# Reordering the prologue of an fp32 transformer block: DMA queue order, and which engine makes which small split

## The reference

```python
mod = silu(c) @ wmod                      # six rows of 128 per batch: sa, ca, ga, sb, cb, gb
h = layernorm(x) * (1 + ca) + sa
q, k, v = h @ (w * scale)                 # 16 heads of 64
a = (q + q_bias) @ k.T / 8 + relative_causal(q @ emb.T / 8)
a = softmax(where(causal, a, -1e9))
x = x + ga * ((a @ v) @ out_kernel + out_bias)
h = layernorm(x) * (1 + cb) + sb
x = x + gb * top1_moe(h)                  # 16 experts, capacity 256, 128 -> 512 -> 128
```

## Time and profile before

| what | value |
|---|---|
| time of the launch, median of 3 runs | 904.1 us (903.34 to 904.54) |
| time of the profiled execution | 906.07 us |
| its span | 904.0 us |
| mean TensorE clock granted | 0.991 |
| PE busy | 875.8 us, 97% |
| ACT busy | 710.3 us, 79% |
| DVE busy | 665.9 us, 74% |
| POOL busy | 518.7 us, 57% |

### The profile page before, as it was taken

One profiled execution on the slowest core, in us unless ns is written; L12 is line 12 of the kernel. 1 busy time (PEld: TensorE's weight loads), 2 busy tenths in 40 slices (PEclk: granted clock), 3 DMA queues, 4 the chain that ended last, 5 costly groups with the idle time before them and its releaser, 6 DMA issues.

```text
span 904.0 us, 17653 instructions
## 1 busy us (share of the span) xinstructions
PE 875.8 (97%) x5632; PEld 702.2 (78%) x5632; DVE 665.9 (74%) x2053; ACT 710.3 (79%) x1970; POOL 518.7 (57%) x786
## 2 busy tenths in 40 slices
PE   6999999999999999999999999999999999997994
PEld 5777777887777778777777877777887777766994
DVE  4778778787878687777878787868777677753884
ACT  4788888888888888888888888888888888841551
POOL 2455555565565755675557556675566556633354
PEclk9899999999999999999999999999999999999998
DMA  7000790000000000000000000000000000006671
GB/s 271 2 1 1 190 243 24 1 19 18 13 1 2 36 1 13 1 28 10 13 1 15 12 13 1 2 21 8 5 1 22 2 13 1 9 22 218 215 213 39
DMA packets 23068, 38.92 MB, mean 43 GB/s; under 512 B 3094, under 2 KB 16135, under 8 KB 22592
## 3 DMA queue, kind: packets, MB, share of 16 engines
q1 hardware_dynamic: 19184, 29.11, 11.1%
q0 software_dynamic: 3072, 5.94, 1.8%
q10 hardware_dynamic: 720, 2.75, 0.9%
HBM read 23.44 MB, written 16.82 MB: 45 GB/s over the span
## 4 chain that ended last, share of the span: by engine, by line
PE 86%; DVE 1%; POOL 1%; DMA 1%; issue 1%; ACT 1%; POOLq 0%; DVEq 0%
PE bank L773 21%; PE bank L803 16%; PE bank L738 15%; PE bank L783 14%; PE bank L810 5%; PE bank L759 4%; PE bank L770 3%; PE bank L981 2%; PE bank L970 2%; DMA x<-xbuf 1%; PE bank L831 1%; POOL out L443 1%; PE bank L961 0%; PE bank L818 0%; PE bank L825 0%
## 5 line engine op out<-in xcount | busy, mean ns | idle before, releaser
L395 POOL TENSOR_SCALAR prob<-prob,rsum 128x128 f32<-128x128 f32 (+3 forms) x512 | 263.1, 532 | 238.4 <-DVE rsum L1101 232.4
L553 ACT ACTIVATE prob<-srow,nmax 128x512 f32<-128x512 f32 (+3 forms) x512 | 286.3, 560 | 66.5 <-DVE nmax L1089 63.7
L1089 DVE CUSTOM_DVE_ANT_0 srow<-bank,consts 128x512 f32<-128x512 f32 (+3 forms) x512 | 247.0, 488 | 98.0 <-issue 76.4
L783 PE MATMUL bank<-consts,prob 128*128 128x128 f32 x1280 | 201.7, 272 | 0.2 <-POOL prob L395 0.2
L783 PEld LDWEIGHTS bank<-consts,prob 128*128 128x128 f32 x1280 | 158.4, 140 | 22.9 <-POOL prob L395 0.5
L388 POOL TENSOR_TENSOR qlo<-qx,qhi 128x384 fp32r<-128x384 f32 x128 | 129.5, 1012 | 54.5 <-ACT qhi L518 53.2
L562 ACT ACTIVATE pt<-bank 128x384 f32<-128x384 f32 x318 | 153.3, 495 | 5.4 <-PE bank L783 5.0
L803 PE MATMUL bank<-pt,v 128*64 128x512 f32 (+3 forms) x1024 | 152.0, 439 | 0.3 <-issue 0.2
L773 PE MATMUL bank<-khi,qhi 128*128 128x512 f32 (+2 forms) x384 | 146.0, 380 | 3.5 <-DVE klo L1112 1.7
L1106 DVE SCALAR_TENSOR_TENSOR qx<-bank,qbias,consts 128x512 f32<-128x512 f32 x128 | 94.2, 736 | 53.6 <-PE bank L738 53.5
L773 PE MATMUL bank<-khi,qlo 128*128 128x512 f32 (+2 forms) x384 | 130.4, 339 | 0.0
(11 more groups left out here) (166 smaller groups left out, 1429.4 us busy)
## 6 DMA issues: line engine op xcount, KB each, us to landing
xbuf<-fill SPq DMA_DIRECT2D x4, 1540.0 KB, 24.4
x<-xbuf SPq DMA_DIRECT2D x16, 385.0 KB, 4.0
raw<-in_w SPq DMA_DIRECT2D x16, 256.0 KB, 8.9
prob<-in_w SPq DMA_DIRECT2D x16, 256.0 KB, 4.7
out<-row SPq DMA_DIRECT2D x8, 256.0 KB, 2.3
x<-in_x SPq DMA_DIRECT2D x1, 1792.0 KB, 13.2
modb<-mod_rows SPq DMA_DIRECT2D x1, 1536.0 KB, 7.8
v<-in_b SPq DMA_DIRECT2D x1, 1024.0 KB, 7.4
```

Source lines behind the costliest of these rows:

```text
L395: end = gp.tensor_scalar(part, part, rsum[:, par, 4 * h + q:4 * h + q + 1], 1.0, ALU.mult, ALU.mult)
L553: act.activation(prob[:, par, h, QOFF[q]:QOFF[q] + P * (q + 1)], srow[:, k % 4, 0:P * (q + 1)], ACT.Exp, bias=nmax[:, par, k:k + 1], scale ...
L783: last = pe.transpose(out[:, n * P:(n + 1) * P], prob[:, par, h, QOFF[q] + k * P:QOFF[q] + (k + 1) * P], ident)
L1089: dve.tensor_tensor_reduce(out=srow[:, k % 4, 0:w], in0=scb[k % 2][:, 0:w], in1=mask[:, S - w:S], scale=-1.0, scalar=BIG, op0=ALU.add, op1 ...
```

## The change

Seven edits, all ahead of or inside the first step:

1. The three later weight loads (`wall` of pairs 1 to 3, `wv`, `wall` of pairs 4 to 7) go from ACT's queue to SP's, behind the tables. `consts` goes ahead of the two `kx` loads.
2. ACT waits for the key table alone (`ktab` at 16); the `kx` loads have a semaphore of their own, on which PE waits.
3. The table's low part goes from POOL (two instructions) to DVE (one of 64x1024), ahead of `vlo`.
4. `low_wq` of pairs 1 to 3 goes from DVE to POOL, ahead of its `low_q`; `low_wv` goes from DVE to POOL, behind `low_wk`.
5. ACT's `high_g` goes ahead of `high_q`, and `high_wv` behind `high_q`; DVE's `low_g` goes ahead of `evac_q`.
6. PE does `w_table(1, 4)` and 8 idle matmuls ahead of the first q projections.
7. PE does `b_table(1, 8)` ahead of the first step and no longer in it.

```diff
@@ SP
             sp.dma_start(h2T[HD:P, :], ktab_d).then_inc(s["ktab"], 16)
+            sp.dma_start(consts[:, 512:], consts_d[:, 128:]).then_inc(s["consts"], 16)
             for h in range(2):
-                sp.dma_start(kx[HD:P, h, :], ktab_d[:, 0:P]).then_inc(s["ktab"], 16)
-            sp.dma_start(consts[:, 512:], consts_d[:, 128:]).then_inc(s["consts"], 16)
+                sp.dma_start(kx[HD:P, h, :], ktab_d[:, 0:P]).then_inc(s["kxt"], 16)
+            sp.dma_start(wall[:, 1:4, :], wall_d[:, 1:4, :]).then_inc(s["wall1"], 16)
+            sp.dma_start(wv, wv_d).then_inc(s["w_v"], 16)
+            sp.dma_start(wall[:, 4:PAIRS, :], wall_d[:, 4:PAIRS, :]).then_inc(s["wall2"], 16)
@@ POOL
-            def low_table():
-
-                gp.wait_ge(s["kt"], 2)
-                gp.wait_ge(s["xn"], 1)
-                for h in range(2):
-                    gp.tensor_tensor(klo[HD:P, h, :], h2T[HD:P, :], khi[HD:P, h, :], ALU.subtract)\
-                        .then_inc(s["kt"], 1)
-                gp.wait_ge(s["kt"], 4)
+            def low_wq(a0, a1, h, after):
+
+                gp.wait_ge(s["whi"], after)
+                gp.tensor_tensor(wlo[q_cols(a0, a1, h)], wall[q_raw(a0, a1, h)], whi[q_cols(a0, a1, h)],
+                                 ALU.subtract).then_inc(s["wlq"], 1)
+
+            def low_wv():
+
+                gp.wait_ge(s["wv"], 1)
+                gp.tensor_tensor(wvlo[:, :], wv, wvhi[:, :], ALU.subtract).then_inc(s["wv"], 1)
...
-            low_table()
+            low_wq(1, 4, 0, 1)
+            low_wq(1, 4, 1, 2)
             low_q(0, 0)
             low_wk(1, 4, 3)
+            low_wv()
             batches(turn)
@@ ACT
             act.dma_start(wmod[:, :, :], wmod_d.rearrange("p (a b) -> p a b", a=6)).then_inc(s["wmod"], 16)
-            act.dma_start(wall[:, 1:4, :], wall_d[:, 1:4, :]).then_inc(s["wall1"], 16)
-            act.dma_start(wv, wv_d).then_inc(s["w_v"], 16)
-            act.dma_start(wall[:, 4:PAIRS, :], wall_d[:, 4:PAIRS, :]).then_inc(s["wall2"], 16)
...
-            act.wait_ge(s["ktab"], 48)
+            act.wait_ge(s["ktab"], 16)
...
             high_wk(1, 4)
+            high_g(1, 4, 3, "whi")
+            high_q(0, 0)
             high_wv()
-            high_q(0, 0)
             evac_k(0, 0)
-            high_g(1, 4, 3, "whi")
             evac_k(0, 1)
@@ PE, first_step and ahead of the steps
-                if k == 1:
-                    pe.wait_ge(s["wall2"], 16)
-                    b_table(1, PAIRS)
...
+            pe.wait_ge(s["wall1"], 16)
+            w_table(1, 4)
+            idle(8)
             pe.wait_ge(s["fhi"], 3)
             pe.wait_ge(s["flo"], 3)
             project_q(0, None, 0, 0)
             project_q(0, None, 0, 1)
-            pe.wait_ge(s["wall1"], 16)
-            w_table(1, 4)
             project_k(0, None, 0)
-            pe.wait_ge(s["ktab"], 48)
+            pe.wait_ge(s["wall2"], 16)
+            b_table(1, PAIRS)
+            pe.wait_ge(s["kxt"], 32)
             pe.wait_ge(s["kt"], 4)
@@ DVE
             dve.tensor_scalar(modT[:, 1:4:2, :], half(2), 1.0, None, ALU.add).then_inc(s["modT"], 1)
+
+            def low_table():
+
+                dve.wait_ge(s["kt"], 2)
+                dve.tensor_tensor(klo[HD:P, :, :], h2T[HD:P, None, :].to_broadcast([HD, 2, S]), khi[HD:P, :, :],
+                                  ALU.subtract).then_inc(s["kt"], 2)
+
+            low_table()
             low(0)
...
-                if k == 0:
-                    low_wv()
...
+            low_g(1, 4, "whi", 4, "wlo")
             evac_q(0, 0, 0)
             evac_q(0, 0, 1)
-            for h in range(2):
-                low_wq(1, 4, h, h + 1)
             low_k(0, 0)
-            low_g(1, 4, "whi", 4, "wlo")
             batches(turn)
```

More of the change, by code:

```diff
@@ L174, in program @@
         mod_dram = nc.dram_tensor("mod_rows", [B, 3 * D], F32).ap()
-        names = ("ident consts open small wall0 wall1 wall2 w_v ktab x0 x1 wmod misc b2 wo zero "
+        names = ("ident consts open small wall0 wall1 wall2 w_v ktab kxt wlq x0 x1 wmod misc b2 wo zero "
                  "e_silu silu wg_mm bias fhi flo whi wlo wlo_k mod_mm modT mev mrow modb gates "
@@ L287, in turn @@
                     sp.wait_ge(s["wlo_k"], 2)
-                    sp.wait_ge(s["wlo"], 6)
+                    sp.wait_ge(s["wlo"], 4)
+                    sp.wait_ge(s["wlq"], 2)
                     sp.wait_ge(s["wv"], 2)
@@ L863, in first_step @@
                     pe.wait_ge(s["whi"], 5)
-                    pe.wait_ge(s["wlo"], 4)
+                    pe.wait_ge(s["wlo"], 2)
                 if k >= 4:
@@ L876, in step @@
                         pe.wait_ge(s["whi"], 4)
-                        pe.wait_ge(s["wlo"], 3)
+                        pe.wait_ge(s["wlo"], 1)
+                        pe.wait_ge(s["wlq"], 2)
                         pe.wait_ge(s["wlo_k"], 1)
@@ L880, in step @@
                         pe.wait_ge(s["whi"], 8)
-                        pe.wait_ge(s["wlo"], 6)
+                        pe.wait_ge(s["wlo"], 4)
                         pe.wait_ge(s["wlo_k"], 2)
@@ L1048, in _ @@
             aggregate(0, 1)
-            def low_wv():
-                dve.wait_ge(s["wv"], 1)
-                dve.tensor_tensor(wvlo[:, :], wv, wvhi[:, :], ALU.subtract).then_inc(s["wv"], 1)
             def low_wq(a0, a1, h, after):
```

## The result

The changed kernel takes 901.79 us (median of 20 runs, 900.11 to 905.40) against 905.37 us for the kernel before in the same sessions (20 runs, 903.34 to 909.56): a ratio of 0.9960, 95% interval 0.9948 to 0.9972, or 3.6 us (2.5 to 4.7). The forecast was 900.1, made on the 904.1 of the first three runs, that is 4.0 us less.

The account below looks back on a forecast made before the run. PE, busy 97% of the span, was taken as the bound. Terms 2.4 + 1.7 - 0.6 + 0.6 - 0.1 to 0.4 gave 3.7 to 4.0 us; 4.0 off 904.1 made 900.1 us, 8-in-10 range 897.7 to 902.6.

Parts of the forecast that it names:

- The chain: Before the projections: with ACT waiting only for the key table, `hn` starts at 10.34 rather than 12.49, 2.15 us earlier.
- `vlo` and POOL: Ahead of the projections: with POOL idle, `vlo` is 0.94 us shorter and ends at 12.5, 3.1 us earlier.
- The loads' landings: Prologue loads: key table there at 5.5 us, `wall` of pairs 1 to 3 at 8.7, last of `wall` at 12.9.
- PE's order: Table (0.74 us) and eight idle matmuls (0.53) ahead of the first projection, which starts at 13.3, 2.4 us earlier.
- `wvhi` ahead of `evac_k`: On ACT, `wvhi` runs to 16.75, so `evac_k` starts 3.5 us earlier, not 4.1: 0.65 lost.
- Tile 5: Fifth score tile of the first step, tile 4 counted from 0: at 23.2 us against 27.32, 4.1 us earlier.
- I take 0.50: First step: PE's granted clock taken at half rate, fifth score tile at 23.2 us; at full rate 22.2.
- given back: First step: if half rate ends as long after the gap, 0.8 us more work runs in it, costing 0.2 to 0.4.
- first rival: Full rate through the first step: fifth score tile at 22.2, projections behind about 1 us more; 898.1 us, chance 0.15.
- third rival: Half rate already from 13.3 us on, through projections and first tiles: 2.7 off the 4.0 us gain, 902.8; chance 0.10.
- All the steps behind move as a block: Steps behind the first: PE is their limit and nothing waits for a clock time, so they keep the whole shift.
- last rival: SP's queue alone is slow, `wall` lands late and PE waits ahead of the first score tile: 909 us, chance 0.05.

Follow-up runs that it names:

- edits12: The kernel before with edits 1 and 2 alone (order of the loads, ACT waiting for the key table alone); ratio 0.9965 to the kernel before.
- wv_hole: The changed kernel with `wvhi` ahead of `high_q` on ACT instead of behind it; ratio 0.9966 to the kernel before.
- best_b: The changed kernel with the later weight loads back on ACT's queue and `wvhi` ahead of `high_q`; 901.06 us, ratio 0.9945 to the kernel before.
- edit2_only_b: The kernel before with edit 2 alone, plus `consts` ahead of `kx` on SP's queue; later weights stay on ACT's queue; ratio 0.9961.
- after_third_b: The changed kernel once more, no edit, on one chip with two of its variants; 901.84 us, ratio 0.9966 to the kernel before.
- less_idle: wv_hole with 14 idle matmuls instead of 30 ahead of batch 0's transposes and none instead of 8 ahead of the first projection; ratio 0.9966.

## Why the prediction was right

- **The chain.** ACT's wait for `kx`, then the table copy, was what stood between the transposes and `hn`. Right, and shown: edit 2 alone gives the gain of the whole, as near as the launch tells. Forecast 0.72 behind the transposes' start, measured 0.76.
- **`vlo` and POOL.** Right: 0.69 once POOL's pair is away, 1.24 where it overlaps, ending each time 0.55 us behind it. The rule of the Trainium skill ("SBUF — State Buffer", Who interferes with whom) fits all of these rows. DVE's table instruction took 1.22 (1.25 taken), POOL's `wvlo` 2.38 (2.9 taken, between bounds of 2.2 and 5.9); the second `low_q` behind it was over at 21.59, 1.7 us ahead of tile 5 (1.4 forecast).
- **The loads' landings.** Too early in the forecast each time: the key table at 7.7 and not 5.5, `wall` of pairs 1 to 3 at 10.8 and not 8.7, the last of `wall` at 15.1 and not 12.9. The sum let the loads land one after the other at the full rate. It cost nothing: the table's copy was over at 8.9, ahead of `hn` at 11.3, and the two parts of `wall` were first read at 12.8 and 16.6. The forecast had left each of them more than 3 us of slack.
- **PE's order.** The table took its full-rate length (the idle matmuls behind it start 0.73 us later, 0.74 taken), and the first projection came 0.45 behind `vlo`, as edit 6 makes it wait. This edit does not shorten what comes before the first tile: from `hn` it is 7.35 us in the changed kernel and 6.96 in edits12 (20.80 - 13.84). What edits 3 to 7 save on top of edits 1 and 2 is later, between tiles 1 and 5: at full rate all through, 4.76 us in edits12 and 3.60 in wv_hole.
- **`wvhi` ahead of `evac_k`.** Right in kind, 0.3 to 0.4 us where 0.65 was taken, since the k projection ended at 16.65 and not at 16.1.
- **Tile 5.** 23.2 forecast, 23.28 measured. That it fits so well is luck, since two misses cancelled: `x` came 0.9 us late, and the rest of the chain was 0.8 quicker than summed (12.75 behind the transposes, 13.58 forecast).
- **The clock.** Before, it was 0.50 in two stretches, 16.9 to 20.3 and 23.7 to 30.5 us; after, in one, 20.3 to 23.7. "I take 0.50" was right up to tile 5 (0.53 from 20.3 to 23.9), the term "given back" wrong in sign: counted from tile 5, half rate ended 0.4 us behind it and not 3.2, and 0.9 us more was won by step 2. That is the later half of the first rival. (The third rival has the first stretch come "about 3 us" behind an idle one; it came 1.2 us behind the end of it, 15.72.) Over all profiles of changed kernels the stretch from 20.3 to 23.9 us was anywhere from 0.53 to 1.00, and it was 1.00 in exactly the five in which the idle matmuls ahead of the transposes had run slowly. Four of these have the changed order, and in them tiles 1 to 5 took 3.6 us and not 4.6: of the 1.4 us that 30 slow idle matmuls cost (3.26 against 1.83), 1.0 came back there. No run varied the one alone.
- **The tail.** Not in the sum: 0.8 us lost at the lower clock in 810 to 820. It goes with the execution: in the third profile of the changed kernel the clock was 0.83 there and nothing was lost (12.24 us between the two rows, 12.25 before). "All the steps behind move as a block" held for the steps and not for what follows them.
- **The queue.** The last rival gave 0.05 to one queue being slow. From 5.0 to 7.5 us less was moved, 277 to 291 GB/s in all eight profiles with the loads on SP's queue against 361 to 389 in all six with them on ACT's: a quarter less, not two thirds. From 7.5 to 13.0 us it was the other way, 370 to 398 against 337 to 344, so one queue is not slow as such. The last part of `wall` was there at 15.1, needed at 16.6. So it cost nothing where I looked, and something where I did not: PE waited for `wmod` in all eight and in none of the six, and the statistics of batch 0 started at 5.51 to 6.86 (mean 6.10) against 5.35 to 6.04 (mean 5.59).
- **The size for the launch.** 4.0 us forecast, 3.6 measured (2.5 to 4.7), with 3.1 to 4.0 in the three measurements. What I missed is that the two halves of the change overlap: each alone gives about 3 us. I had summed only the whole, so the sum stood, but a reader would have credited each edit with its own term. And the size is in part luck: +0.9 us from the clock ahead of step 2 and -0.5 from there to the end of the span were both not in the sum.

Still open in part: why the launch gains 3 to 4 us where step 2 starts 5 to 6 us earlier in the profiles. From step 2 to the end of the span took 868.45 us before and 868.9 to 869.4 in the three profiles of the changed kernel: that is 0.5 to 0.9 of it. Another 0.7 is that the profiled execution of before is that much above the median of its launches (906.07 against 905.37). It had at least 9.6 us of half rate ahead of step 2 (3.0 and 6.6); whether its other executions had as much is not known, since only one profile of it was taken.

## What to carry to other kernels

Look for the semaphore that counts several loads where the waiting engine reads only one: splitting it was worth as much here as seven edits together, as near as the launch tells. Test the halves of a change alone where all of it works on one chain, since their terms may overlap. And a padding of idle matmuls is work in the queue: sized at full rate, it ran at half rate in 4 of the 13 profiles with 30 of them and held the transposes back, and cutting it to 14 did not help either.

## What the runs showed of the hardware that was not expected

- **The early loads came at another rate with another queue.** From 5.0 to 7.5 us the DMAs moved 361 to 389 GB/s with the later weights on ACT's queue and 277 to 291 with all of them on SP's (six and eight profiles). The Trainium skill ("DMA: Bandwidth & Descriptors", Issuing engines are not separate DMA queues) has all queues run on the same engines, with only the time of issuing to be saved; the measured rates differ all the same. But two more things differ with the queue. The time of issuing is one: the three later loads were asked for at 1.65 to 2.62 us on ACT's queue and at 4.48 to 5.60 on SP's. What moves in the stretch is the other: tables in short rows alone, or long weight rows between them. The DMA engines were no less busy (a share of 1.08 to 1.13 against 1.00 to 1.07), and from 7.5 to 13.0 us the same eight kernels moved more than the six (370 to 398 GB/s against 337 to 344). That speaks for the order of the rows and not for the queue; it was not parted.
- **The idle matmuls' rate goes with the wait ahead of them.** In the five profiles where PE had waited 0.94 us or more for `wmod`, the padding behind it ran at half rate; in the nine with 0.57 us or less, at full rate. All five have the loads on SP's queue. It is a coincidence of rows; no run varied the wait alone.
- **The 63 steps take one of two lengths.** From the first attention output to the last it was 757.73 us before, 757.97 after, but 759.04 in best_b, whose two ends are below; edits12, edit2_only_b, after_third_b and less_idle had 758.8 to 759.1 too, the remaining seven 757.7 to 757.8. The difference builds up by about 0.2 us in each batch from the second on, at a granted clock of 1.00. The changed kernel itself is in both groups (757.97 and 757.72, but 759.13 in after_third_b), so it belongs to the execution and not to the change, and it is a third of what was to be measured.

```profile
42.39 0.60 ACT L572 ACTIVATE ohi<-bank 128x512 fp32r<-128x512 f32 x1
801.43 0.60 ACT L572 ACTIVATE ohi<-bank 128x512 fp32r<-128x512 f32 x1 [2.52 <-PE bank L808]
```
